# A spline feed-forward block: the feature reads split by block of 128 inner units instead of by kind of feature

## What is computed

```python
x = x + attention(layernorm(x), Wq, Wk, Wv, Wo)          # causal, 16 heads
x = x + ffn(layernorm(x), gate_cp, up_cp, down_cp)       # first feed-forward
x = x + gla(layernorm(x), Wq, Wk, Wog, Wig, g_weight)    # gated linear attention, a scan over tokens
x = x + ffn(layernorm(x), gate_cp, up_cp, down_cp)       # second feed-forward, same weights

def ffn(h, gate_cp, up_cp, down_cp):
    gate_w = spline_reconstruct(gate_cp, 1024, 256)      # weights are cubic splines through about
    up_w   = spline_reconstruct(up_cp, 1024, 256)        # 2,000 control points each
    down_w = spline_reconstruct(down_cp, 256, 1024)
    inter = silu(h @ gate_w.T) * (h @ up_w.T)
    return inter @ down_w.T
```

## Time and profile before

| | us |
|---|---|
| median of 3 runs | 969.03 (968.34 to 973.57) |
| the profiled execution | 972.26 |
| its span, first to last instruction | 970.5 |
| PE busy in it | 803.6 (83%) |
| DVE busy | 632.1 (65%) |
| ACT busy | 502.4 (52%) |
| POOL busy | 237.2 (24%) |

### The profile page before, as it was taken

One profiled execution on the slowest core, in us unless ns is written; L12 is line 12 of the kernel. 1 busy time (PEld: TensorE's weight loads), 2 busy tenths in 40 slices (PEclk: granted clock), 3 DMA queues, 4 the chain that ended last, 5 costly groups with the idle time before them and its releaser, 6 DMA issues.

```text
span 970.5 us, 19870 instructions
## 1 busy us (share of the span) xinstructions
PE 803.6 (83%) x6676; PEld 684.8 (71%) x6676; DVE 632.1 (65%) x1272; ACT 502.4 (52%) x967; POOL 237.2 (24%) x306
## 2 busy tenths in 40 slices
PE   4689999999999987778677759999997686678768
PEld 4468777777777764667666658899986476667757
DVE  7565777777777774556555447788887365566545
ACT  2155454554555555445444336588885354445433
POOL 3922222232323232100000001266665300000000
PEclk9687999999999998688788889999999598899889
DMA  5945676575766537867778870000004778988881
GB/s 174 116 72 68 124 106 93 89 97 90 99 86 90 78 60 142 159 143 141 142 140 137 143 94 1 1 0 0 0 1 103 143 137 157 154 149 177 159 155 45
DMA packets 64997, 98.67 MB, mean 102 GB/s; under 512 B 7153, under 2 KB 28050, under 8 KB 64898
## 3 DMA queue, kind: packets, MB, share of 16 engines
q1 hardware_dynamic: 64940, 97.95, 58.3%
HBM read 41.82 MB, written 30.41 MB: 74 GB/s over the span
## 4 chain that ended last, share of the span: by engine, by line
PE 41%; DMA 37%; SPq 9%; DVE 5%; issue 3%; POOL 3%; ACT 3%; ACTq 0%; POOLq 0%; DVEq 0%
DMA stk<-fx 27%; DMA fx<-fs 8%; PE bank L412 6%; SPq L561 5%; PE bank L413 4%; PE bank L414 4%; PE pair_a L850 4%; PE bank L864 3%; PE pair_b L819 3%; PE pair_b L1159 2%; PE bank L1159 2%; PE pair_a L1124 1%; POOL spline L649 1%; PE pair_b L831 1%; PE bank L868 1%
## 5 line engine op out<-in xcount | busy, mean ns | idle before, releaser
L1820 DVE TENSOR_TENSOR inter<-gact,pair_b 128x512 f32<-128x512 f32 x128 | 87.4, 683 | 116.4 <-ACT gact L1407 113.7
L412 PE MATMUL bank<-wd_hi,in_hi 128*128 128x256 f32 x512 | 155.9, 304 | 8.4 <-DVE X L1831 5.3
L413 PE MATMUL bank<-wd_lo,in_hi 128*128 128x256 f32 x512 | 153.7, 300 | 0.0
L414 PE MATMUL bank<-wd_hi,in_lo 128*128 128x256 f32 x512 | 153.7, 300 | 0.0
L1071 PE MATMUL pair_a<-stk,cst 126*128 126x512 f32 x128 | 59.9, 468 | 102.1 <-DMA stk<-fx 102.1
L1280 ACT ACTIVATE prob<-pair_a 128x768 f32<-128x768 f32 x128 | 103.7, 810 | 69.7 <-PE pair_a L850 68.5
L1407 ACT ACTIVATE gact<-pair_a 128x512 f32<-128x512 f32 x128 | 75.2, 587 | 121.6 <-PE pair_a L1071 121.5
L1653 DVE TENSOR_REDUCE mx<-pair_b 128x6 f32<-128x768 f32 x124 | 118.1, 953 | 28.5 <-PE pair_b L831 27.4
L639 POOL TENSOR_SCALAR_AFFINE_SELECT prob<-prob 128x512 f32<-128x512 f32 x128 | 81.8, 639 | 217.5 <-ACT prob L1280 217.5
L1825 DVE TENSOR_TENSOR in_lo<-inter,in_hi 128x512 fp32r<-128x512 f32 x128 | 89.0, 696 | 63.4 <-ACT in_hi L1415 62.6
L1415 ACT ACTIVATE in_hi<-inter 128x512 fp32r<-128x512 f32 x128 | 80.6, 630 | 92.8 <-DVE inter L1820 85.5
(11 more groups left out here) (226 smaller groups left out, 1966.0 us busy)
## 6 DMA issues: line engine op xcount, KB each, us to landing
stk<-fx SPq DMA_DIRECT2D x144, 224.0 KB
stack<-stage SPq DMA_DIRECT2D x192, 128.0 KB, 4.7
fx<-fs SPq DMA_DIRECT2D x48, 512.0 KB, 4.0
X<-in_attn_a_x SPq DMA_DIRECT2D x14, 256.0 KB, 5.1
result<-X SPq DMA_DIRECT2D x7, 512.0 KB, 17.0
stack<-mrow SPq DMA_DIRECT2D x128, 4.0 KB
wdx<-spline SPq DMA_DIRECT2D x1, 1024.0 KB
wd_lo<-wdx SPq DMA_DIRECT2D x16, 64.0 KB
```

Of the source, the lines that this page charges most:

```text
L412: pe.matmul(dst, l_hi, r_hi, start=first, stop=False)
L413: pe.matmul(dst, l_hi, r_lo, start=False, stop=False)
L414: return pe.matmul(dst, l_lo, r_hi, start=False, stop=last)
L1820: dve.tensor_tensor(inter[:, m % 2, :], gact[:, m % 2, :], pair_b[:, m % 2, :], ALU.mult).then_inc(f_.up, 1)
```

## The change

It has two parts. First, the transfers. `fx` now holds three full copies of the rows (high, low, high), so that the 126 rows of a block lie at regular distances, and `read` has one transfer for each block, 126 partitions of 2 KB, instead of one for each kind and part, 14 partitions of 16 KB. The third copy is written by transfers of its own. The moments' writes cover 126 rows, not 128. Second, the order in which the first pairs of the second feed-forward are made ready. A part of the diff that only changes the semaphores' counts (48 to 96, 144 to 16 * MT) is left out.

```diff
-FROWS = 3 * FSTEP + 5
+FROWS = 3 * FSTEP
-        fx = nc.dram_tensor("fx", [2, FROWS, 2 * S], F32, kind="Internal").ap()
+        fx = nc.dram_tensor("fx", [3 * FROWS + P, 2 * S], F32, kind="Internal").ap()
...
+            copies = fx[0:3 * FROWS, :].rearrange("(v q) t -> v q t", q=FROWS)
+                def write(slot, at, n):
+                    sp.dma_start(copies[0:2, at:at + n, :].rearrange("v p t -> p v t"),
+                                 fs[0:n, :, slot, :].bitcast(F32)).then_inc(f_.fw, 16)
+                    sp.dma_start(copies[2, at:at + n, :], fs[0:n, 0, slot, :].bitcast(F32)).then_inc(f_.fw, 16)
 # write_x
                     for c in range(CT):
-                        sp.dma_start(fx[:, P * c:P * c + P, :].rearrange("v p t -> p v t"),
-                                     fs[:, :, c, :].bitcast(F32)).then_inc(f_.fw, 16)
+                        write(c, P * c, P)
 # write_moments
-                    at = 2 + 2 * FSTEP
-                    sp.dma_start(fx[:, at:at + P, :].rearrange("v p t -> p v t"),
-                                 fs[:, :, CT, :].bitcast(F32)).then_inc(f_.fw, 16)
+                    write(CT, 2 + 2 * FSTEP, P - 2)
 # read
-                    for n, part in enumerate((0, 1, 0)):
-                        for r in range(3):
-                            rows = fx[part, 2 + FSTEP * r:2 + FSTEP * r + P, :]
-                            rows = rows.rearrange("(m s) t -> s m t", s=KG)[0:NB]
-                            at = NF * n + NB * r
-                            sp.dma_start(stk[at:at + NB, u].bitcast(F32), rows).then_inc(f_.ld, 16)
+                    for m in range(MT):
+                        at = 2 + KG * m
+                        rows = fx[at:at + 9 * FSTEP, :].rearrange("(r q) t -> r q t", q=FSTEP)[:, 0:NB, :]
+                        sp.dma_start(stk[0:NFX, u, m, :].bitcast(F32), rows).then_inc(f_.ld, 16)
 # PE, feed-forward period
+                        if not prev:
+                            first(m)
                         if m == 2 and nxt2:
...
-                        if not prev and m > 1:
-                            first(m)
 # PE, GLA period: turns and moments of pair 1
-                    if at == B - 1:
+                    if at == B:
                         pe.wait_ge(f_.ml, upto(f_.ml, PAIRS, 1))
-                        f2_turn(1, 0, bank_t)
-                    if at == B:
-                        f2_moments(1, bank_t)
+                        f2_turn(1, 1, bank_t)
...
-                    if at == B - 1:
-                        pe.wait_ge(g_.qs, upto(g_.qs, n, 1))
-                        pe.wait_ge(g_.kt, upto(g_.kt, n, 1))
-                        f2_turn(1, 1, bank_p)
...
+                    if at == B - 1:
+                        pe.wait_ge(g_.qs, upto(g_.qs, n, 1))
+                        pe.wait_ge(g_.kt, upto(g_.kt, n, 1))
+                        f2_turn(1, 0, bank_p)
 # last_output_used (PE), last_output (ACT), last_residual (DVE): moments of pair 1
+                if m == 0:
+                    f2_moments(1, bank_t)
+                if m == 1:
+                    f2_high_moments(1, bank_t)
+                if m == 1:
+                    f2_low_moments(1, bank_t)
 # DVE, GLA period
-                    if at == B - 1:
-                        f2_low_moments(0, bank_t)
                     if nxt3:
...
                     if at == B - 1:
-                        f2_low_x(1, 0, bank_t)
+                        f2_low_moments(0, bank_t)
...
-                    if at == B - 2:
+                    if at == B - 3:
                         f2_stats(1)
```

29 lines of the change are left out of this document (14 added, 15 removed).

## The result

The changed kernel takes 896.75 us (median of 4 runs, 894.24 to 902.62). Beside it, the kernel before took 971.3 (968.34 to 975.9). The ratio is 0.9237, with a 95% interval of 0.9174 to 0.93, so it is 7.6% faster. The forecast was 889, in a range of 855 to 930. The profiled execution took 902.62, its span 900.9.

What follows compares the result with a forecast made beforehand. Transfers were taken to bound both feed-forwards, a write plus a read for each pair. Savings of 46.3 us in the first and 34.1 in the second (80.4) took 972.3 to 891.9, or 889 for a median; range 855 to 930.

Steps and rivals of the forecast that it cites:

- What bounded the kernel, and what made packets slow: Both feed-forwards: writes and reads in turn set the pace, 26.4 us a loop; few target partitions make packets slow.
- Nine engines: New reads: nine engines share a transfer, 24.3 GB/s each, 219 together, data in 9.4 us; chance 0.58 near full speed.
- A read: Read of `stk` in both feed-forwards: 12.0 us for 20.7, ends 8.7 and 23.0; issues 0.61 us each.
- A write: Write of `fx` for each pair, now three copies: 8.7 us for 6.3, ends 7.8 and 10.2.
- The loop: Write plus read for each pair: 20.7 us for 26.6 in the first feed-forward, 21.9 in the second; PE's work 19.2.
- the store: Second feed-forward: storing a result, 0.52 MB, shares the read's time and adds 1.3 us, so the loop is 21.9.
- first start: First feed-forward: first read lands at 389.4; PE waits for the attention's last residual, starts at 390.9 for 396.3.
- The new order: GLA's end: low moments 2.1 us later, write 0.9 longer; moments of pair 1 then cost 0.6 before the second read.
- PE as the bound: Rival, both feed-forwards: 14 to 16 engines make reads 8.7 us, PE's 19.2 decides, 861 us in all; chance 0.20.
- Nine engines at 18 GB/s: Rival, reads: 15.3 us each, loops 24.0 and 25.2, 35 us gained, 934 in all; chance 0.12.
- The slower case: Rival, reads: reading DRAM limits each engine to 11.2 GB/s, read 23.0 us, loop 31.7, 1057 in all; chance 0.07.
- The signs: Expected in the profile: periods 20 to 22 us, PE's `stk` wait 15 to 30, SP's write waits longer, read waits shorter.

Runs made afterwards that it cites:

- old_targets: The changed kernel's new `fx` and writes, but nine reads into 14 partitions each; doesn't compute the layer: 1009.24 us, ratio 1.0384 to the kernel before.
- old_source: The changed kernel with fourteen engines a read and the new 126-partition targets, but DRAM rows at the old distances; doesn't compute the layer: 872.97 us, ratio 0.8982.
- no_third_copy: The changed kernel with the third copy written only for the first pair of each feed-forward, so later results are wrong: 872.06 us, ratio 0.8957.
- spread_down_rows: Fourteen engines a read and two `fx` in turn (865.62 us), plus `wd_lo<-wdx` in eight transfers of 128 partitions, not sixteen of 8: 860.99 us.
- old_place: The changed kernel with the second feed-forward's first groups put back in the old order, so the new transfers alone: 897.66 us, ratio 0.9237.

## Why the forecast was right, and where its sizes were off

**What bounded the kernel, and what made packets slow: right.** The forecast read from three rows that few target partitions make slow packets. *old_targets* and *old_source* show it, with source and target moved apart.

**Nine engines: right.** Share 0.58 and 206 GB/s, forecast "near 0.6 and 200 to 220". An engine carries 21 to 24 GB/s (22.9 in the stretch shown) for the forecast's 24.3; at 206 GB/s the data take 10.0 us and not 9.4.

**A read: 12.9 us for 12.0.** Of the 0.9, some 0.6 is the engine's rate, and 0.3 the rest. The old read of 20.7 us, from which the forecast took what a read has beside its data, was one of the longer ones (mean 19.9). With the mean write of 6.3 it would make an old loop of 27.0 and not of 26.4; the means of both, 19.9 and 6.3, make 26.2 for a period of 26.6. The issues are dearer than forecast:

```profile
L563 SPq DMA_DIRECT2D stk<-fx x128: 723/724/891, 380.9 to 869.6; - x128
```

That is 0.72 us (with the gaps 6.2 for eight) for 0.61, taken from another transfer of unlike sides. Under 10 us of data it costs little; with fourteen engines it shows.

**A write: 8.3 to 9.8 us, mean 8.9, for 8.7.** *no_third_copy* gives the third copy some 2.2 us (8.4 for 6.2), forecast 2.4. The six issues take 4.6 us or more, where three took 1.8 and the forecast had 2.6; that they lie under the data at this length too isn't shown. One term was overlooked: the moments' writes of 126 partitions run at 287 to 309 GB/s, share 0.88, for 371 and 1.02. 0.77 MB at 300 in place of 380 is 0.5 us.

**The loop: 21.7 for 20.7, and 21.9 for 21.9.** In the first feed-forward the sum was 1.0 short, by read and write. In the second it came out exactly, but by luck, out of two errors: the store was to add 1.2, and the two feed-forwards differ by 0.2.

**Where 80.4 became 69.0.** Point by point, forecast and measured shift in us:

| | forecast | measured | from |
|---|---|---|---|
| first start | -5.4 | -2.0 | 396.28 to 394.28 |
| its first period | -5.4 | -3.1 | 25.0 to 22.0 |
| six periods | -35.5 | -29.6 | 159.7 to 130.1 |
| to the second feed-forward's first start | -5.8 | -7.3 | 183.9 to 176.6 |
| its first period | -3.8 | -2.8 | 25.2 to 22.4 |
| six periods | -24.5 | -24.3 | 155.8 to 131.5 |
| sum (unrounded) | -80.4 | -69.0 | |

The mis-sized term is the loop in the first feed-forward: 5.9 us of the 11.4. The second is the start: PE waited there for the attention's last residual, as forecast, but that came later than in the profile before. DVE in the changed kernel:

```profile
393.23 0.69 DVE L1694 TENSOR_TENSOR X<-bank,X 128x512 f32<-128x512 f32 x1 [1.79 <-PE bank L414]
```

393.23 for 390.19. The forecast took the attention's end as unchanged. Two steps ahead of that end can be told apart in ACT's timeline; the second of them, before and in the changed kernel:

```profile
376.43 1.09 ACT L1398 ACTIVATE fs<-pair_b 128x512 fp32r<-128x512 f32 x2 [1.18 <-DMA fx<-fs]
380.87 1.08 ACT L1401 ACTIVATE fs<-pair_b 128x512 fp32r<-128x512 f32 x2 [2.64 <-DMA fx<-fs]
```

The first is the landing of `wd_lo<-wdx`: ACT goes on at 372.94 for 369.96, 3.0 us. *spread_down_rows* shows that this landing does set the attention's end. That it came 3.0 later looks like scatter between executions: ACT goes on at 368.0 to 370.0 in the three kernels with the old writes and at 366.7 to 373.0 in the ten with the new ones. The second is the write of pair 0, which must have left `fs` before ACT fills it again. This wait, shown above, is 1.2 us in all three kernels with the old writes and 2.6 in all ten with the new ones, so 1.4 us are a cost of the new writes, and the forecast had nothing for it. In this profile the shift is 4.1 us at ACT's last row of the attention (390.12 for 385.98) and 3.0 at the residual. PE made up 1.1 between: its granted clock was 1.00 there (391 to 393) and 0.50 in the profile before (389 to 391).

The residual alone doesn't explain the start. The first read was issued at 380.92, for 377.4 in the forecast, because the moments it needs come out of ACT behind the same landing (their write at 376.60, for 373.61 before). It landed by 393.75, and the residual was done at 393.92, so either would have held PE.

The medians differ less: the profiled execution is the slowest of its four (902.62, median 896.75), and for the median the forecast was 7.8 short. Between the medians the gain was 74.5 us (971.3 to 896.75).

**The new order: right in direction, smaller in size.** It was to cost 2.1 us from the GLA's products to the first read, and 0.6 behind that. Measured is 11.2 for *old_place*'s 10.0, so 1.2. The write, which was to cost 0.9 there, costs 1.6 (10.0 for 8.4 before), so that the whole is 11.2 where 11.4 was forecast. In DVE's timeline the low moments come 6.3 us after the products:

```profile
705.42 0.69 DVE L1815 TENSOR_TENSOR fs<-bank,fs 128x512 fp32r<-128x512 f32 x1 [0.21 <-ACT fs L1405]
```

where 7.6 was forecast. The moments of pair 1 let the second read start 9.3 us after the first gate matmul (722.97 to 732.30), and 9.3 was forecast (759.1 to 768.4).

**The rivals.** PE as the bound came at 19.2 us a period in the forecast and 861 in all; with fourteen engines it is 19.6, and 869.7. That floor holds PE's stalls behind DVE's addition to X; what it would be without them wasn't tried. Nine engines at 18 GB/s: refuted by 21 to 24. The slower case: refuted by *old_source* and by the rate itself.

**The signs.** Most came as named. PE's wait for `stk` is 35.5 us, above the 15 to 30. SP's waits for the reads fell from 223 to 95 us, as said, but those for the writes did not rise (58 before, 55 now): SP spends the longer write on issuing it.

## What to carry to other kernels

A DMA share near 1 doesn't say that a transfer is fast: divide the rate by the busy engines, and if an engine carries a third of what it does elsewhere (7.9 for 23 GB/s), look at how many partitions the transfer writes. Then look at the sizes of the first dimension on both sides, for they set how many engines work: here one more reordering of the rows, nine first to fourteen first, was worth 3% for nothing but permuted columns, and the same look at a load outside the loop brought 0.5 to 1.4%. And where a loop is a write plus a read, a shorter write, a shorter read and an overlap all ran into the same floor of compute here; take the cheapest one, and don't expect them to add.

## What was not expected of the hardware

- Overlap with a transfer into few partitions brings little. With it in flight the share is 0.98 to 1.03 and the engines carry 128 to 155 GB/s together, for 112 of the read alone and 358 of the write once it was over.
- An issue's price on SP goes with the shape: 0.39 us (median) for a read of 14 partitions on both sides, 0.72 for nine groups into 126 partitions, 0.79 for fourteen groups into 126, though the same number of bytes is moved by each of the last two. With fourteen engines, issuing takes 6.7 of a read's 10.9 us.
- An engine of fourteen carried 19 to 20 GB/s, one of nine or seven 21 to 24. Why wasn't tried. Slower filling by SP's issues isn't the whole of it: with fourteen, behind the last issue (446 to 448), it is still 263 GB/s at a share of 0.85, 19 an engine.
- Spread over 126 partitions, a row distance in DRAM of the old or the new kind made no difference (9.9 to 10.8 us for a read with the old one, 10.4 to 11.0 with the new one).
